# First mixture stored in table order by plain DMAs, parts gathered by indirect DMAs in the pair attention

## The reference, cut to what matters

```
x = x + FFN0(Attention0(x, bias, mask))        # 16 heads, then a ternary linear layer
c = MoE1(x, cond)                              # first mixture
x = x + Block(c)                               # pair attention + second mixture

MoE1: scores = softmax(logits)                 # 8 experts, 128 hidden features
      two experts per token, weights normalised
      y[t] = sum over the two: weight * (leaky(x Wg) * (x Wu)) Wd
      y   += a shared expert of 256 hidden features
Block(c), c taken as [S, B=2, D]:
      a = c + proj(attention over the pair of tokens)     # 16 heads of 16, causal
      g = softmax(layernorm(a) Wr); two of 8 experts
      out = a + sum over the two: g * gelu(l Wup) Wdown   # 512 hidden features
```

## Time and profile before

| | before |
|---|---|
| median of three runs | 1079.36 us |
| profiled execution, its time | 1077.8 us |
| span in the profile | 1077.8 us, 22664 instructions |
| PE busy | 930.0 us (86%) |
| DVE, ACT, POOL busy | 799.7, 735.9, 610.6 us |
| attention, feed-forward | 0 to about 723 us |
| first mixture | 723 to 800 us |
| pair attention | 800 to 928 us |
| second mixture | 928 to 1078 us |

### The profile page before, as it was taken

How to read it: one execution, slowest core, us unless ns; L and a number is a source line. 1 busy time by engine, 2 the same in 40 slices (tenths; PEclk the granted TensorE clock), 3 DMA queues, 4 the chain that set the end, 5 groups by cost and what they waited for, 6 DMA issues and landing times. The chain is left out here.

```text
span 1077.8 us, 22664 instructions
## 1 busy us (share of the span) xinstructions
PE 930.0 (86%) x6178; PEld 811.2 (75%) x6178; DVE 799.7 (74%) x2315; ACT 735.9 (68%) x1651; POOL 610.6 (57%) x745
## 2 busy tenths in 40 slices
PE   7899999999999999999999849678753882499996
PEld 5578888888888998988888637568752662399995
DVE  7579989899898998988888798465458776244443
ACT  2278888888888998989989656235564552466663
POOL 2368878777676676755555364544572147244444
PEclk8889999999999999999999969799976885699998
DMA  9166666667566666665666031348926013444453
GB/s 308 38 184 182 177 179 181 177 175 199 156 189 198 179 190 179 192 205 165 192 175 199 28 133 42 115 147 270 320 86 196 21 69 133 107 77 78 76 82 45
DMA packets 110549, 162.83 MB, mean 151 GB/s; under 512 B 15993, under 2 KB 84089, under 8 KB 109402
## 3 DMA queue, kind: packets, MB, share of 16 engines
q1 hardware_dynamic: 99272, 142.16, 44.6%
q0 software_dynamic: 10560, 19.18, 7.8%
q10 hardware_dynamic: 594, 0.04, 0.0%
HBM read 110.63 MB, written 25.53 MB: 126 GB/s over the span
## 5 line engine op out<-in xcount | busy, mean ns | idle before, releaser
L2154 POOL TENSOR_SCALAR probs<-probs,inv_sum 128x1024 f32<-128x1024 f32 (+3 forms) x128 | 301.4, 2368 | 172.9 <-DVE inv_sum L2305 172.9
L2287 DVE TENSOR_TENSOR pT_lo<-t_ps,pT_hi 128x512 fp32r<-128x512 f32 (+1 forms) x320 | 202.8, 634 | 21.1 <-ACT pT_hi L2182 20.6
L2200 ACT ACTIVATE probs<-probs,neg_max 128x1025 f32<-128x1025 f32 (+7 forms) x256 | 197.6, 772 | 29.9 <-DVE neg_max L2265 28.6
L2369 PE MATMUL t_ps<-ident,probs 128*128 128x128 f32 x1152 | 180.3, 275 | 1.1 <-DVE pT_lo L2287 1.1
L2182 ACT ACTIVATE pT_hi<-t_ps 128x512 fp32r<-128x512 f32 (+1 forms) x320 | 175.3, 549 | 6.4 <-PE t_ps L2369 3.2
L2389 PE MATMUL o_ps<-pT_hi,values 128*128 128x256 f32 x576 | 174.8, 323 | 5.3 <-DVE pT_lo L2287 3.5
L2265 DVE CUSTOM_DVE_ANT_0 probs<-s_ps,bias_set,neg_null 128x512 f32<-128x512 f32 (+3 forms) x256 | 164.3, 642 | 4.5 <-PE s_ps L2338 2.8
L2369 PEld LDWEIGHTS t_ps<-ident,probs 128*128 128x128 f32 x1152 | 142.2, 141 | 31.3 <-DVE pT_lo L2287 3.1
L2390 PE MATMUL o_ps<-pT_lo,values 128*128 128x256 f32 x576 | 150.2, 280 | 0.0
L2337 PE MATMUL s_ps<-k_hi,q_hilo 128*128 128x512 f32 (+3 forms) x384 | 143.1, 373 | 4.7 <-DVE neg_max L2265 1.5
L2338 PE MATMUL s_ps<-k_lo,q_one 128*128 128x512 f32 (+3 forms) x384 | 134.4, 350 | 0.0
(11 more groups left out here) (348 smaller groups left out, 2135.3 us busy)
## 6 DMA issues: line engine op xcount, KB each, us to landing
bias_set<-bias_dram SPq DMA_DIRECT2D x16, 1024.0 KB, 5.4
bias_set<-bias_dram SPq DMA_DIRECT2D x16, 896.0 KB, 5.4
bias_set<-bias_dram SPq DMA_DIRECT2D x16, 768.0 KB, 4.9
bias_set<-bias_dram SPq DMA_DIRECT2D x16, 640.0 KB, 4.7
q_hilo<-q_hi SPq DMA_DIRECT2D x128, 64.0 KB, 2.0
q_hilo<-q_lo SPq DMA_DIRECT2D x128, 64.0 KB, 2.0
q_one<-q_hi SPq DMA_DIRECT2D x128, 64.0 KB, 2.0
bias_set<-bias_dram SPq DMA_DIRECT2D x16, 512.0 KB, 5.5
```

Source lines behind the costliest of these rows:

```text
L2154: last = pool.tensor_scalar(keys, keys, inv_sum[:, x.set, unit, h:h + 1], None, ALU.mult)
L2200: act.activation(p, p, ACT.Exp, scale=-1.0, bias=neg_max[:, x.set, row.unit, h:h + 1], accum_out=row_sum[:, x.set, row.unit, h:h + 1]).the ...
L2287: dve.tensor_tensor(pT_lo[n % 3][:, 0:count, :], t_ps[TURNS["slot", n] % 3][:, 0:2 * P * count].rearrange("p (n q) -> p n q", n=count), pT ...
L2369: last = pe.transpose(t_ps[at % 3][:, P * (2 * m + h):P * (2 * m + h) + P], probs_row(x, row, h)[:, 1 + P * (k + m):1 + P * (k + m) + P], ...
```

## The change

1. The first mixture's tile i is stored whole, as it stands, to rows 128 i of `parts` by a plain DMA of SP (issued behind the reload of tile i + 16). POOL only waits for the stores. The 8 destination words leave the rows: a row has 265 words.
2. Where a token's part stands is computed instead: its row in the slab minus the first row of its expert's slab plus 128 x the expert's first tile. The ranks and next rows of all tokens are kept, `make_table`'s small tensors are computed on all partitions, and DVE's `locate` makes `parts_at` in the first three steps of the mixture.
3. The pair attention gathers: POOL issues, for each group and part, four indirect DMAs of 128 rows (32 in all), between its powers, each part buffer when it is free.
4. Five of the eight weight loads stay in the mixture, one every fifth tile; those of experts 7, 6 and 4 are issued by SP in the pair attention after `second_added` 1, 2, 3. `weights_high(5)` and `weights_low(5)` stand later, and DVE's adds, moments and shifts are in another order.

```
-PART_ROWS = TOP * T + P * (E + SPARES)
+PART_ROWS = ROUTED * P
+SPLIT = [0, 1, 2, 3, 5, 7, 6, 4]
+FIRST_LOADED = SPLIT[:5]
+LAST_LOADED = SPLIT[5:]
@@ feed-forward, top_weights
-                dve.scalar_tensor_tensor(rt.all_rows[:, mine, DEST:ID].bitcast(I32), rt.rank[:, 0:BT, :], float(T),
-                                         rt.ids[:, mine].unsqueeze(2).broadcast_to([P, BT, E]), ALU.mult, ALU.add)
@@ first mixture, SP
+            at = []
+            for g in range(R // BUFS, WORDS):
+                at.extend(nc.values_load_multi_w_load_instructions(rt.row_of[0:1, BUFS * g:min(BUFS * (g + 1), ROUTED)],
...
             sp.wait_ge(summed, SUMMED)
...
-                for i in these:
-                    sp.wait_ge(scaled, i - R + 1)
-                    sp.wait_ge(dest_ready, i - R + 1)
-                    sp.dma_start(rows[i % R], routed_rows[bass.ds(at[i % BUFS], P), :]).then_inc(rows_in[i % R], 16)
-                    if (i - R) % W2_EVERY == 0 and (i - R) // W2_EVERY < E:
-                        load_expert((i - R) // W2_EVERY)
+            for i in range(ROUTED):
+                sp.wait_ge(scaled, i + 1)
+                if i + R < ROUTED:
+                    sp.dma_start(rows[i % R], routed_rows[bass.ds(at[i], P), :]).then_inc(rows_in[i % R], 16)
+                sp.dma_start(parts[P * i:P * i + P, :], y[i % BUFS]).then_inc(out_stored[i % BUFS], 16)
+                if i % W2_EVERY == 0 and i // W2_EVERY < len(FIRST_LOADED):
+                    load_expert(FIRST_LOADED[i // W2_EVERY])
@@ first mixture, POOL
-            for i in range(AHEAD):
-                address(i)
-            for i in range(ROUTED):
...
-                pool.indirect_dma_start(parts, bass.IndirectOffsetOnAxis(ap=dest[:, i % BUFS:i % BUFS + 1], axis=0),
-                                        y[i % BUFS], None).then_inc(out_stored[i % BUFS], 16)
             for k in range(BUFS):
                 pool.wait_ge(out_stored[k], 16 * ((ROUTED + BUFS - 1 - k) // BUFS))
@@ first mixture, DVE (locate(n) ends step n)
+            def locate(part):
+                first = rt.first_row[:].unsqueeze(1).broadcast_to([P, NT, E])
+                if part == 0:
+                    dve.scalar_tensor_tensor(chosen_first[:, :, 0, :], rt.rank[:], 0.5, first, ALU.is_lt, ALU.mult)
+                    dve.scalar_tensor_tensor(chosen_first[:, :, 1, :], rt.rank[:], 1.0, first, ALU.is_equal, ALU.mult).then_inc(located, 1)
+                elif part == 1:
+                    dve.wait_ge(located, 1)
+                    dve.tensor_reduce(shift[:], chosen_first[:], AX.X, ALU.add).then_inc(located, 1)
+                elif part == 2:
+                    dve.wait_ge(located, 2)
+                    dve.tensor_tensor(rt.parts_at[:], rt.next_rows[:], shift[:], ALU.subtract).then_inc(located, 1)
@@ pair attention, SP
-            for k in range(BUFS):
-                sp.wait_ge(out_stored[k], 16 * ((ROUTED + BUFS - 1 - k) // BUFS))
-            for n in range(TOP * GROUPS):
-                load_part(n // TOP, n % TOP)
+            for n, e in enumerate(LAST_LOADED):
+                sp.wait_ge(second_added, n + 1)
+                sp.dma_start(w2[:, e, :].bitcast(F32), aps["m2_w"][e]).then_inc(late_in[e], 16)
@@ pair attention, POOL
+            def gather(g, k):
+                n = TOP * g + k
+                if n >= PARTS:
+                    before, slot = divmod(n - PARTS, TOP)
+                    pool.wait_ge(second_added if slot else first_added, before + 1)
+                for j in range(GROUP):
+                    b, i = divmod(j, COUPLES)
+                    at = tile(g, j)
+                    pool.indirect_dma_start(part[n % PARTS][:, b, i, :], None, parts,
+                                            bass.IndirectOffsetOnAxis(ap=rt.parts_at[:, at, k:k + 1], axis=0)).then_inc(parts_in[n % PARTS], 16)
...
+            for k in range(BUFS):
+                pool.wait_ge(out_stored[k], 16 * ((ROUTED + BUFS - 1 - k) // BUFS))
+            pool.wait_ge(located, 3)
+            gather(0, 0)
+            gather(0, 1)
+            gather(1, 0)
+            gather(1, 1)
             power(0, 0)
+            gather(2, 0)
+            gather(2, 1)
             power(0, 1)
+            gather(3, 0)
+            gather(3, 1)
             power(0, 2)
             power(0, 3)
@@ pair attention, DVE
             shifts(0, 0)
             add_part(1, 1)
             moments(0, 1)
+            shifts(0, 1)
             add_part(2, 0)
-            add_part(2, 1)
-            shifts(0, 1)
-            moments(0, 2)
-            add_part(3, 0)
-            add_part(3, 1)
             differences(0)
             products(0)
             scores(0)
             peaks(0)
-            shifts(0, 2)
+            add_part(2, 1)
+            moments(0, 2)
             probabilities(0)
             weigh(0)
             attend(0)
-            moments(0, 3)
+            add_part(3, 0)
+            shifts(0, 2)
             differences(1)
             products(1)
             scores(1)
             peaks(1)
-            weights_low(5)
+            add_part(3, 1)
+            moments(0, 3)
             probabilities(1)
             weigh(1)
             attend(1)
             add_projected(0)
             moments(1, 0)
             shifts(0, 3)
             shifts(1, 0)
+            weights_low(5)
             sum_up(0)
```

More of the change, by code:

```diff
@@ L37 @@
 EARLY = 2
-DEST = D + E
-ID = DEST + E
+ID = D + E
 ROW = ID + 1
@@ L944, in pair_attention_stage @@
         parts_in = [sem(f"pa_parts_in{i}") for i in range(PARTS)]
+        late_in = {e: sem(f"pa_w_in{e}") for e in LAST_LOADED}
         var_ready, rstd_ready, shift_ready, normed = ([sem(f"pa_{n}{norm}") for norm in range(2)]
@@ L973, in _ @@
         def _(sp):
-            def load_part(g, k):
-                n = TOP * g + k
-                if n >= PARTS:
-                    before, slot = divmod(n - PARTS, TOP)
-                    sp.wait_ge(second_added if slot else first_added, before + 1)
-                tiles = parts[T * k:T * k + T, :].rearrange("(n p) d -> p n d", p=P)
-                for b in range(B):
-                    at = QT * b + COUPLES * g
-                    sp.dma_start(part[n % PARTS][:, b], tiles[:, at:at + COUPLES, :]).then_inc(parts_in[n % PARTS], 16)
-            for k in range(BUFS):
-                sp.wait_ge(out_stored[k], 16 * ((ROUTED + BUFS - 1 - k) // BUFS))
-            for n in range(TOP * GROUPS):
-                load_part(n // TOP, n % TOP)
+            for n, e in enumerate(LAST_LOADED):
+                sp.wait_ge(second_added, n + 1)
+                sp.dma_start(w2[:, e, :].bitcast(F32), aps["m2_w"][e]).then_inc(late_in[e], 16)
             sp.dma_start(out[T:OUT_ROWS, :].rearrange("(n p) d -> p n d", p=P),
@@ L1302, in weights_high @@
                 e = SPLIT[s]
-                act.wait_ge(w_in[e // 2], w_used + 32)
+                if e in LAST_LOADED:
+                    act.wait_ge(late_in[e], 16)
+                else:
+                    act.wait_ge(w_in[e // 2], w_used + 16 * sum(other // 2 == e // 2 for other in FIRST_LOADED))
                 if e == 7:
@@ L1327, in _ @@
             first_norm(1, 1)
-            weights_high(5)
             exponentials(0)
@@ L1338, in _ @@
             first_norm(2, 1)
+            weights_high(5)
             turned_attn(1, 0)
@@ L1653, in _ @@
                 hidden_low(n + 1)
+                locate(n)
         @block.tensor
@@ L2844, in program @@
                                                                    (ln1_w, ln1_b, ln2_w, ln2_b, w_qkv, w_router), loaded,
-                                         rows, rows_in, inputs.w_raw, done, out_stored, second_words, w2_lo_ready), rt, routed_rows, parts, out)
+                                         rows, rows_in, inputs.w_raw, done, out_stored, located, second_words, w2_lo_ready), rt, routed_rows, parts, out)
                     middle.close()
```

95 lines of the change are left out of this document (38 added, 57 removed).

## The result

Measured over 20 runs each, the kernel after takes 1088.95 us (median; 1081.1 to 1095.04) and the kernel before 1084.33: ratio 1.0052, 95% interval 1.0033 to 1.0071. That is 5.6 us slower by the ratio; the two medians lie 4.6 apart. The forecast was 1085.0 against 1079.36, a ratio of 1.0052.

A forecast was written before the change was run, and what follows sets the result against it. The first mixture was taken as held by POOL's scatter bursts, not PE alone; afterwards POOL's gather queue bounds. +18.8 (gathers) - 11.7 (mixture) - 0.3 + 0.7 = +7.5 us on 1077.8 gives 1085; range 1073.5 to 1098.

The forecast's parts named there:

- M: End of the first mixture's last scaled tile: forecast to move from 800.2 to 788.5, a gain of 11.7 us.
- The couples: First mixture, two tiles each: 2.74 us per couple if all stalls go, against 3.85 before.
- the hold by the reloads: First mixture: reloads, stores and weight loads, 11.4 MB at 334 GB/s, hold PE about 3 us.
- The cause of the stalls: First mixture: ACT's 21.1 us of waits for up products laid on POOL's back-to-back scatters, as an inference.
- rival (b): Pair attention: gathers cost 1.56 us like accumulating scatters, 16 us more, total 1101; chance 0.12.
- the holding by additions: Pair attention: seven further add_part on DVE each hold a POOL gather some 0.8 us, smaller ones a little; 5.6 us.
- Power(0, 2): Pair attention, POOL: the power behind the last gather, set at 1.06 us, ending at M + 57.0.
- attend(1): Pair attention, DVE: ends at M + 65.0 instead of M + 46.2, +18.8 us from the queue of gathers.
- rival (a): Faster: DVE does not hold the gathers and the mixture runs unheld at 2.74; total 1072; chance 0.27.
- The rest: Small DVE instructions leaving the feed-forward stage, -0.3 us, and weights_low(5) moved behind shifts(1, 0), +0.7 us.
- Signs: Right: no ACT wait for L1684 over 1 us; wrong: attend(1) to second mixture's first product changed by over 2 us.
- case (d): The forecast itself: stalls gone, POOL's queue the new bound, total 1079 to 1090; chance 0.47.

The follow-up runs named there:

- first pair: The first profiled traces of the kernel before and the kernel after; ratio of after to before 1.0052.
- c2_after: Kernel after run again unchanged, on the same chip as c1_before; ratio to before 1.0062.
- e2: Kernel after, but POOL's indirect scatter stores each first-mixture tile to the same rows instead of SP's plain DMA; ratio to before 1.0149.
- e4: Kernel before with only the weight loads of the kernel after (five in the mixture, three in the pair attention); ratio to before 0.9998.
- kind B: One of two kinds of traces, seen on two chips, with the kernel before at 1051 to 1053 us; whether chip or time decides is not shown.
- c1_before: Kernel before run again unchanged, for its trace beside the kernel after on the same chip; ratio to before 0.9973.
- e3_plain_parts: Kernel after without the 32 gathers: SP loads the parts in plain DMAs, giving wrong results; ratio to before 0.9908.
- kind A: The other kind of traces, seen on two chips and in the first runs, with the kernel before at 1081 to 1086 us.
- second pair: Both kernels run again unchanged on one chip, c1_before and c2_after; ratio of after to before 1.0062.
- e6: Kernel after, but POOL instead of SP issues the plain stores of the first mixture's tiles; one run, no ratio given.
- e1: Kernel after, but SP reads the 23 row numbers in three batches, each just ahead of its reloads; ratio to before 1.0022.

## Why the prediction was right

The path was right: the stalls of the mixture went, and a queue of gathers on POOL cost more than they had. That forecast and measured ratio agree to four digits is luck; the interval alone reaches from 0.33 to 0.71%, and the median of before moved by 5 us between its first three runs and twenty.

**The mixture.** Forecast: M 11.7 us earlier. F to M is 11.8 shorter in the first pair and 12.6 in the second. The couples run at 2.74, as said. SP's first reload slipped by 1.2 us (F + 13.6 against F + 12.4), not by 3; the hold by the reloads, put at 3 from the bytes and 334 GB/s, was 3.5 in one stop (5.6 in c2_after). The trace of after is near that rate and below the 425 GB/s that the Trainium skill gives for one large load ("DMA: Bandwidth & Descriptors", section Bandwidth): in full stretches of after (share 0.99 and 1.01) it moved 320 and 341.

```profile
750.00:760.00 10.00, 6.43 (x40) 5.96 (x40) 3.09 (x8) 3.01 (x8) 0.00 (x0) 0.83 0.99 320
...
770.00:780.00 10.00, 10.00 (x90) 10.00 (x88) 6.91 (x15) 7.29 (x18) 0.00 (x0) 1.00 1.01 341
```

**The cause of the stalls.** Laid on the scatters by their place in time alone; e2 and e4 show it. What I had not allowed for is that it does not happen in every set of runs: on kind B the same scatters of the feed-forward stage delay nothing.

**The gathers.** The first was forecast at M + 3.9 and came at M + 3.7; the fifth out at M + 13.9, it was 13.8. A free gather is 0.95 and 0.30, as the scatters of the earlier trace rows: rival (b), 1.56, falls. The term that was mis-sized is the holding by additions: 5.6 forecast, 3.5 measured over the 27 gathers (those at 821.23, 825.28, 835.36 and 841.64 took 0.3 to 1.1 more than 0.95). Power(0, 2) took 1.90 where 1.06 was set (and three of 1.06 are 3.2, not the 3.3 of the sum). So power(0, 2) ended at M + 54.9, not 57.0, and attend(1) at M + 63.6, not 65.0. That DVE's two-input instructions hold the gathers, from which rival (a) would have freed them, is plain: each of the first five ends 0.8 to 0.9 after one split ends. The Trainium skill says so too ("SBUF — State Buffer", section on the two separate sides): a Vector instruction with two SBUF inputs keeps the port pair that it shares with GpSimd for its whole length, against a GpSimd instruction that reads SBUF. The trace agrees, with splits of 2.22 us and gathers, whose row numbers stand in SBUF.

**The rest.** Forecast +0.4; from attend(1) to the end it was -1.2 in the first pair and +4.4 in the second. In c2_after DVE begins to read PE's last router product 4.1 us late, at 912.55 for an end of 908.45, in c1_before 0.04 late. After has this delay too (6.2 us, above) and e3_plain_parts (5.5), the other five traces of kind A and all of kind B don't (0.04). So on kind A the tail can lose some of what the mixture gained. Why the first pair still shows -1.2 with such a delay in after is not explained: the +0.4 was not tested by any run.

**Signs.** Two that I had named came out otherwise. ACT does wait over 1 us for up products (3.45 as the pipeline fills, 1.32 behind the stop for rows), and attend(1) to S is 3.8 longer in the second pair, where over 2 was to count against me. PE is idle until M + 31.9, as said.

Sum: +7.5 was forecast, the spans from F to the end give +4.5 and +9.8, the ratios +5.6 and +6.7. The forecast's case (d) is what happened, on kind A. On kind B I would have been wrong: by the estimate above little or none of the 11.7 us of gain is there to be had, and the variants of after measured there stand 11 to 23 us above before.

## What to carry to other kernels

A transfer that moves from an indirect store behind the work to indirect loads ahead of it is no longer hidden: count the issues (32 at 1.25 us) as one queue and see what stands in it. Before a stall is sold as the gain of a change, look at the same stage on more than one chip: here the stall was worth about 12 us in the runs of kind A and, by an estimate, little or nothing in those of kind B. And where a stage is fed at the DMA engines' rate, try the order of the transfers (small, urgent ones ahead of the 1 MB ones) before an earlier start: in one trace each, the first took PE's longest wait for rows to 0.95 us, and the second left waits of 2.1 and 2.7.

## What the runs showed of the hardware that I had not expected

- Two kinds of runs: the same kernel before at 1081 to 1086 us or at 1051 to 1053 us. In the first, PE's completions are seen 1 to 8 us late while POOL scatters back to back (20 to 26 of them in the mixture), in the second none; gathers back to back delayed none in either.
- A gather of 128 rows of 1 KB costs POOL the same 0.95 us as a scatter, and a plain store of a tile issued by POOL 0.54 us (e6, L1558 over 39 stores; least, median and most in ns, first and last start):

```profile
L1558 POOL DMA_DIRECT2D parts<-rt_rows x39: 539/539/613, 726.2 to 781.2; - x39
```

- An earlier start of the reloads made the mixture no shorter (e1: 66.3 against 62.8 and 64.5).
